# The closing pass of a four-layer graph network moved into the blocks of its last graph convolution

## What is computed

```python
def gcn_conv(x, src, dst, W, b):            # dinv = 1/sqrt(degree)
    h = x @ W
    msg = h[src] * (dinv[src] * dinv[dst])[:, None]
    return segment_sum(msg, dst) + b
# h3 is the layer's normalised input, x3 the residual stream
x_out = x3 + gcn_conv(relu(gcn_conv(h3, ..., W1, b1)), ..., W2, b2)   # 64 -> 32 -> 64 features
```

## Time and profile before

| | |
|---|---|
| median of 3 runs | 7401.49 us (7392.78 to 7404.23) |
| profiled execution, span from first to last instruction | 7386.2 us |
| DVE / PE / GpSimd / ACT busy over the span | 61 / 63 / 51 / 22 % |
| mean granted TensorE clock | 0.816 of full speed |
| second graph convolution, first sums to last addition | 6716.4 to 7214.6 us |
| closing pass | 7214.6 to 7386.2 us |

### The profile page before, as it was taken

One profiled execution on the slowest core, in us unless ns is written; L12 is line 12 of the kernel. 1 busy time (PEld: TensorE's weight loads), 2 busy tenths in 40 slices (PEclk: granted clock), 3 DMA queues, 4 the chain that ended last, 5 costly groups with the idle time before them and its releaser, 6 DMA issues. The chain is left out here.

```text
span 7386.2 us, 101314 instructions
## 1 busy us (share of the span) xinstructions
PE 4675.6 (63%) x31722; PEld 4192.0 (57%) x31722; DVE 4503.1 (61%) x5720; ACT 1623.3 (22%) x2242; POOL 3795.4 (51%) x3348
## 2 busy tenths in 40 slices
PE   4665335760188785555555866666668774784797
PEld 2354334650177785555555866666568774674675
DVE  6998443222577786666667842232398894683457
ACT  0143112330143343222222421111134340000001
POOL 0198565563277403777771047777600006766766
PEclk9866668995599998766767987777789996997899
DMA  2298666656722374332333753334357883122009
GB/s 75 48 276 259 140 147 140 138 108 201 252 73 73 101 245 154 83 79 79 81 78 101 249 164 109 109 109 112 100 186 250 304 307 112 49 59 91 14 12 278
DMA packets 837873, 1024.59 MB, mean 139 GB/s; under 512 B 589119, under 2 KB 601812, under 8 KB 836380
## 3 DMA queue, kind: packets, MB, share of 16 engines
q1 hardware_dynamic: 534716, 742.63, 31.5%
q0 software_dynamic: 144256, 90.12, 8.3%
q10 hardware_dynamic: 158560, 187.31, 7.6%
HBM read 608.19 MB, written 417.84 MB: 139 GB/s over the span
## 5 line engine op out<-in xcount | busy, mean ns | idle before, releaser
L839 POOL DMA_INDIRECT gc_msgs<-t,src_rows x784 | 754.4, 962 | 1098.1 <-POOLq L146 804.2
L893 POOL DMA_INDIRECT acc<-de_sums,de_put x392 | 608.5, 1552 | 410.9 <-DMA acc<-de_sums,de_put 263.5
L1913 PEld LDWEIGHTS gc_ring<-gc_msgs,gc_hot 128*128 128x128 f32 x4736 | 628.4, 210 | 305.9 <-issue 298.1
L1913 PE MATMUL gc_ring<-gc_msgs,gc_hot 128*128 x4736 | 654.9, 297 | 230.4 <-SPq L1872 229.3
L839 POOL DMA_INDIRECT at2s_ends<-h,src_rows x392 | 369.9, 944 | 533.6 <-POOLq L146 414.4
L839 POOL DMA_INDIRECT at1s_ends<-x,src_rows x392 | 389.2, 993 | 490.5 <-POOLq L146 371.3
L1027 PE MATMUL de_ring<-de_win,de_pick 128*128 x2368 | 343.2, 305 | 272.7 <-DMA de_win<-t 272.7
L1027 PEld LDWEIGHTS de_ring<-de_win,de_pick 128*128 128x128 f32 x2368 | 322.9, 217 | 295.0 <-issue 289.1
L839 POOL DMA_INDIRECT at1s_ends<-x,dst_rows x392 | 419.0, 1069 | 119.5 <-issue 119.5
L839 POOL DMA_INDIRECT re_rows<-x,src_rows x392 | 406.5, 1037 | 125.1 <-issue 124.8
L1393 PE MATMUL re_psR<-w_rel,re_own 128*128 128x128 f32 x3136 | 398.6, 293 | 73.6 <-DVE re_own L1330 73.3
(11 more groups left out here) (471 smaller groups left out, 11359.4 us busy)
## 6 DMA issues: line engine op xcount, KB each, us to landing
rew_win<-x SPq DMA_DIRECT2D x74, 544.0 KB, 4.0
at1w_win<-g SPq DMA_DIRECT2D x74, 544.0 KB, 4.0
at2w_win<-g SPq DMA_DIRECT2D x74, 544.0 KB, 4.0
de_near<-same SPq DMA_DIRECT2D x74, 512.0 KB, 5.1
de_win<-t SPq DMA_DIRECT2D x74, 512.0 KB, 4.6
x<-rew_win SPq DMA_DIRECT2D x74, 512.0 KB, 2.9
h<-at1w_win SPq DMA_DIRECT2D x74, 512.0 KB, 2.9
h<-at2w_win SPq DMA_DIRECT2D x74, 512.0 KB, 2.9
```

What stands on the lines that cost most here:

```text
L839: nc.gpsimd.indirect_dma_start(buf[:, t * width:(t + 1) * width], None, table, bass.IndirectOffsetOnAxis(ap=rows[:, t:t + 1], axis=0)).the ...
L893: nc.gpsimd.indirect_dma_start(g.acc0[j % 2], bass.IndirectOffsetOnAxis(ap=put[:, j:j + 1], axis=0), sums[:, j * D:(j + 1) * D], None, com ...
L1913: done = nc.tensor.matmul(ring[:, bass.ds(to[n], SLOT)], hot[k][:, n, :], each_group(msgs[:, bass.ds(of[n], MID)], SLOT // MID), start=Fal ...
```

## The change

- `skip_dense` adds the last bias `bg2` to `x` on GpSimd, after `centred`; ACT's store of `x3` waits for it (`biased`).
- `gcn_last` takes the place of `gcn_edges("gc2")` and of `gcn_close`. It does the same 74 blocks. The ring is now two halves of 8 slots (2 banks each), cleared by ACT instead of PE; PSUM also holds one transposed and one widened block. Per iteration m, PE does the sums of block m, transposes the 16 tiles that are finished after block m-1, and widens the ones transposed before; DVE does hot(m), two half additions of block m-1, the scaling by `dinv`, and `close(m-1)`; ACT clears two halves, evacuates the transposes, loads an `x` block and stores a closed one. A block of 16 tiles starts where the path stands, so tiles at the seam may be written twice, in order.
- The output is laid out by partition; the host puts it in node order.
- `setup` makes the slot addresses of the halves and two more columns of `g.blocks` (six small DVE operations).

```diff
+++ setup
+                link(v.tensor_scalar(half[:, 0:HALF], at[:, 0:HALF], float(SLOT), None, ALU.mult))
+                link(v.tensor_scalar(half[:, HALF:S], at[:, HALF:S], at[:, HALF:HALF + 1], None, ALU.subtract))
+                link(v.tensor_scalar(half[:, HALF:S], half[:, HALF:S], float(SLOT), float(HALF * SLOT), ALU.mult, ALU.add))
...
+++ skip_dense
+            @block.gpsimd
+            def _(pool):
+                def bias(b):
+                    s = b.slot
+                    held(pool, centred, b.number + 1, g.passed)
+                    nc.gpsimd.tensor_tensor(grouped(x[s][:, :], D), grouped(x[s][:, :], D), each_group(g.w["bg2"][:, :], J), ALU.add).then_inc(biased, 1)
+                pipeline(pool, bias, slots=DEEP)
...
-                    act.wait_ge(centred, b.number + 1)
+                    act.wait_ge(biased, b.number + 1)
...
+++ gcn_last, ACT
+                def clear(unit):
+                    if unit >= 2:
+                        act.wait_ge(added, unit - 1)
+                    nc.scalar.activation(ring[:, unit % 2 * BUF:(unit % 2 + 1) * BUF], blank[:, :], ACT.Copy).then_inc(zeroed, 1)
...
+                for m in range(BLOCKS + 1):
+                    if m < BLOCKS:
+                        clear(2 * m)
+                        clear(2 * m + 1)
+                    if m >= 1:
+                        turn(m)
+                    if m >= 2:
+                        if m + 1 <= BLOCKS:
+                            load(m + 1)
+                        store(m - 1)
+                store(BLOCKS)
...
+++ gcn_last, PE
+                def turn(m):
+                    pe.wait_ge(scaled, m)
+                    if m >= 2:
+                        pe.wait_ge(evac, m - 1)
+                    transpose_pairs(nc, psT, u[m % 2], g.ident, S // 4).then_inc(turned, 1)
+
+                def widen(m):
+                    pe.wait_ge(evac, m)
+                    if m >= 2:
+                        pe.wait_ge(ready, m - 1)
+                    times(nc, psH, uT[m % 2], g.w["gcn2"], S // 4).then_inc(product, 1)
+
+                for m in range(BLOCKS):
...
+                    pe.wait_ge(hot_made, m + 1)
+                    need = pe.value_load(g.blocks[m:m + 1, 1:2], min_val=1, max_val=STEPS)
+                    pe.wait_ge(arrived, need)
+                    for n in range(S):
+                        if n % HALF == 0:
+                            pe.wait_ge(zeroed, 2 * m + n // HALF + 1)
+                        done = nc.tensor.matmul(ring[:, bass.ds(to[n], SLOT)], hot[m % 2][:, n, :],
+                                                each_group(msgs[:, bass.ds(of[n], MID)], SLOT // MID),
+                                                start=False, stop=(n % HALF == HALF - 1), skip_group_check=True)
+                        if n % HALF == HALF - 1:
+                            done.then_inc(summed, 1)
+                    if m >= 1:
+                        turn(m)
+                    if m >= 2:
+                        widen(m - 1)
+                turn(BLOCKS)
+                widen(BLOCKS - 1)
+                widen(BLOCKS)
...
+++ gcn_last, DVE
+                def close(m):
+                    dve.wait_ge(x_in[m % 3], 16 * ((m - 1) // 3 + 1))
+                    dve.wait_ge(product, m)
+                    v.tensor_tensor(x[m % 3][:, :], x[m % 3][:, :], psH[:, :], ALU.add).then_inc(ready, 1)
+
+                for m in range(BLOCKS + 1):
+                    if m < BLOCKS:
+                        if m >= 2:
+                            dve.wait_ge(summed, 2 * (m - 1))
+                        v.tensor_tensor(hot[m % 2][:, :, :], each_group(fixed[:, 0:P], S), spread(g.steep[:, m * S:(m + 1) * S], P),
+                                        ALU.is_equal).then_inc(hot_made, 1)
...
+                    for h, col in enumerate((0, 6)):
+                        unit = 2 * (m - 1) + h
...
+                        dve.wait_ge(summed, unit + 1)
...
+                        v.tensor_tensor(grouped(window, MID), grouped(window, MID),
+                                        grouped(ring[:, h * BUF:(h + 1) * BUF], SLOT)[:, :, 0:MID], ALU.add).then_inc(added, 1)
...
+                    v.tensor_tensor(grouped(u[m % 2][:, :], MID), grouped(ended, MID), dinv, ALU.mult).then_inc(scaled, 1)
+                    if m >= 2:
+                        close(m - 1)
+                close(BLOCKS)
```

More of the change, by code:

```diff
@@ L1956, in _, with gcn_last @@
                         nc.vector.scalar_tensor_tensor(grouped(o[:, :], MID), grouped(o[:, :], MID), 0.0, dinv, ALU.max, ALU.mult).then_inc(done_made, 1)
[L1959 to L1971, removed]
-        with nc.Block() as block:
+def gcn_last(nc, g, nodes, acc, out):
+    W = B * MID
+    BUF = HALF * SLOT
+    with Room(nc, g, "gc2") as r:
+        msgs = r.sb("msgs", [P, T * MID])
+        hot = [r.sb(f"hot{k}", [P, S, P]) for k in range(2)]
+        blank = r.sb("blank", [P, BUF])
+        x = [r.sb(f"x{k}", [P, S * D]) for k in range(3)]
+        u, uT = ([r.sb(f"{n}{k}", [P, S * MID]) for k in range(2)] for n in ("u", "uT"))
+        ring, fixed = r.ps("ring", [P, 2 * BUF]), r.ps("fixed", [P, 512])
+        psT, psH = r.ps("psT", [P, S * MID]), r.ps("psH", [P, S * D])
+        got = [r.sem(f"got{k}") for k in range(4)]
+        x_in = [r.sem(f"x_in{k}") for k in range(3)]
+        acc_in, done_out = r.sem("acc_in"), r.sem("done_out")
+        arrived, blanked, hot_made, zeroed, summed, added, link_s, scaled, turned, evac, product, ready = (r.sem(n) for n in (
+            "arrived", "blanked", "hot_made", "cleared", "summed", "added", "link", "scaled", "turned", "evac", "product", "ready"))
+        with nc.Block() as block:
+            @block.gpsimd
+            def _(pool):
+                for b in range(STEPS):
+                    if b >= 4:
+                        held(pool, arrived, b - 3, g.passed)
+                    gather(nc, msgs[:, b * W:(b + 1) * W], nodes, g.src_rows[:, b * B:(b + 1) * B], got[b % 4])
@@ L1973, in _ @@
             @block.sync
             def _(sp):
[L1975 to L1980, removed]
+                for k in range(4):
+                    part = slice(k * (PITCH // 4) * MID, (k + 1) * (PITCH // 4) * MID)
+                    sp.dma_start(acc[:, part], nodes.rearrange("(p t) d -> p (t d)", t=PITCH)[:, part]).then_inc(acc_in, 16)
@@ L1982, in _ @@
             @block.vector
             def _(dve):
[L1984 to L2018, removed]
-                        act.dma_start(out[CHUNK * (STEPS - 1):N - LAST_REST, :].rearrange("(j p) d -> p j d", p=P),
-                                      grouped(x[b.slot][:, 0:LAST_FULL * D], D)).then_inc(last_out, 16)
-                        act.dma_start(out[N - LAST_REST:N, :], x[b.slot][0:LAST_REST, LAST_FULL * D:(LAST_FULL + 1) * D]).then_inc(stored[b.slot], 16)
-                        act.wait_ge(last_out, 16)
-                    else:
-                        act.dma_start(whole[b.number], grouped(x[b.slot][:, :], D)).then_inc(stored[b.slot], 16)
-                def landed(b):
-                    act.wait_ge(stored[b.slot], 16 * b.nth)
-                    act.sem_inc(free, 1)
-                pipeline(act, order=[(0, turn), (2, store), (4, landed)], slots=DEEP)
@@ L2031, in _ @@
-            @block.gpsimd
-            def _(pool):
-                def bias(b):
-                    s = b.slot
-                    held(pool, x_in[s], 16 * b.nth, g.passed)
-                    nc.gpsimd.tensor_tensor(grouped(x[s][:, :], D), grouped(x[s][:, :], D), each_group(g.w["bg2"][:, :], J), ALU.add).then_inc(biased, 1)
-                pipeline(pool, bias, slots=DEEP)
+                v = nc.vector
+                link = Link(dve, link_s)
+                v.memset(blank[:, :], 0.0).then_inc(blanked, 1)
```

82 lines of the change are left out of this document (74 added, 8 removed).

## The result

The changed kernel takes 7851.99 us (median of 4 runs, 7848.21 to 7854.65) against 7402.86 (7392.78 to 7418.66) before: a ratio of 1.0598, with an interval of 1.058 to 1.0616. It is slower by 449 us, and the forecast was 7853.

A forecast was written before the change was run, and what follows sets the result against it. PE, and early the gathers, bounded the convolution. In the changed kernel a ring through PE, DVE and ACT: 6743.0 + 965.6 + 23 + 1.7 + 105 = 7838, plus 15.3: 7853 us; range 7810 to 7896, for 8 in 10 7700 to 7905.

The forecast's parts named there:

- The ring: gcn_last: close, comparison, addition, clear, sums, transposes and product follow one another, 11.8 us, 13.6 with clock; 71 blocks 965.6 us.
- The clock: gcn_last: PE's idle of 5.2 us per block lowers its granted clock afterwards, costing 1.8 us a block.
- The exclusion: skip_dense: POOL's bias addition starts first and holds small multiplication L1830 for 2.2 us, 48 times: +105 us.
- the reading of L752: Dense stage: L752, said to have two SBUF operands, ran 1.22 us undisturbed inside a POOL addition; by it alone, 0 us.
- the ring without the exclusion: Rival: gcn_last's ring as forecast, but L1830 in skip_dense not held by POOL; 7753 us, chance 0.37.
- The tail: End of gcn_last: last sums, transposes, products, closes, additions, clock and final store take 23 us.
- The new operations of the setup: setup: six small DVE operations, each near 0.17 us plus a gap, +1.7 us (0 to 3).
- ACT's loads and stores: gcn_last: x loads and stores on ACT's queue, two issues of about 0.4 us per block, are hidden: 0.
- DVE has more than half of each block free: Second graph convolution before the change: only PE and, early, the gathers set the pace; ACT is wholly free.
- The offset of 15.3 us: Whole kernel: median of the runs lies 15.3 us above the profiled span, kept and added to 7838 for 7853.
- The low-clock rival: gcn_last: low clock for much of PE's work, 16 us a block, +170, about 8020 us; chance 0.06.
- The faster rival: gcn_last: comparison and close overlap PE's sums, so a block costs 7.5 us; 7313 us, chance 0.04.

The follow-up runs named there:

- PE kept busy: Changed kernel plus 20 products of zeros on PE at the start of each last-stage block, in its idle time: 7738.52 us.
- the comparison ahead: Changed kernel with DVE making the comparison for block m+1 before close(m-1) instead of after it: 7669.47 us.
- the run with one input: Changed kernel with skip_dense's 16-element multiplication by dinv replaced by a reciprocal with one SBUF operand: 7760.66 us.
- The kernel with the ring opened: Changed kernel with DVE doing close(m-2), then comparison m+1, and ACT loading x for m and storing m-2: 7445.06 us.
- the last one: The kernel with the ring opened, plus skip_dense's bias waiting for the previous chunk's result and ACT's x store one step deeper: 7352.54 us.

## Why the prediction was right, and which step of it was wrong

**The ring** was right in order and size: 13.6 us forecast, 13.67 in the block shown and 13.62 in the mean. From the close to the start of the sums it was taken as 5.15 us and took 5.09 (7406.98 to 7412.07). Two errors cancel in PE's part. At full clock it was taken as 6.6 us (4.0, 0.60, 1.99) and takes 6.11 from the sums to the next close (7305.66 to 7311.77, with PE kept busy). Some 0.2 of these 0.5 us lie in the 4.0 us of the sums, which the prediction says leave out the blanking of the ring: the one product at L1912 stands between the 24 and the 8 instructions of the earlier trace rows, and without it 32 take 3.83 us. The clock was taken as 1.8 us and cost 2.5 in the block shown (8.58 us from 7412.07 to 7420.65, less 6.11). That 13.6 was met so closely is in this part luck. The tests by order are the stronger evidence: with the comparison ahead 182 us go, with the close deeper too 407 go.

**The exclusion** was right in size: 105 forecast, 100.1 measured, because the wait is 2.06 us longer per chunk and not 2.2. In six chunks POOL led by 0.02 us and the multiplication took 2.37, as forecast; in the 42 others it started 0.18 us after DVE's end, not 0.29, and led by 0.13.

**The step that was wrong** is the reading of L752. The prediction says that it had "also two SBUF operands" and that it does not agree with the rule of the Trainium skill (SBUF — State Buffer, "SBUF: two separate sides"). It had one in SBUF and one in PSUM. By that rule a GpSimd operation that reads SBUF and a DVE operation with two SBUF inputs exclude each other, and the one that starts second waits; every row here agrees: L761, L1987 and L1844 held, L752 held in both runs that put its operand in SBUF, and free with it in PSUM. L1994 and L1848, with one operand in PSUM, are free too. The chance of 0.37 for the ring without the exclusion rested on that misreading and on the near tie of the starts; with the right one the case against 105 us would have been only the question who starts first. It did not spoil the forecast, because the value was taken from L761, the nearest row.

**The rest.** The tail took 24.8 us (23 forecast). The new operations of the setup cost about 1 us where they stand (1.7 forecast): from L482 to the first write of the first dense stage's `cen` it takes 223.2 to 223.8 us in the three traces without them and 223.9 to 225.0 in the seven with them. ACT's loads and stores and the longer output rows were taken as 0, and no wait of the stage names them; the output rows alone were shown to be worth nothing. The difference of the spans is 460.2 us (452 forecast), of which 10.6 belong to neither part and have no shown cause. The prediction's sentence that DVE has more than half of each block free holds for the mean of the stage (212 of 498 us busy) and not for the late block of the earlier trace rows, where it works 2.98 of 5.29 us; nothing in the sum hangs on it. The offset of 15.3 us was too large a correction: the span of the profiled execution after lies only 5.6 us under the median of its runs. The forecast of the span was 8 us too low and the offset 10 us too high, so that the errors cancel to 1 us in the median, which is luck.

**The rivals.** The ring without the exclusion is measured by the run with one input: 7760.66, against 7753 worked out. The low-clock rival fell (13.6 us a block and not 16, with a granted clock of 0.75 in the stage). The faster rival's condition, that neither comparison nor close holds PE, was not met by this order. The kernel with the ring opened and the last one meet it: the comparison lies under PE's sums and the close beside ACT's clear. Its 7313 us left out the 105 of the exclusion, although nothing in the rival removes it: with the term the same sum gives 7418, and the kernel with the ring opened, which has the exclusion, took 7445.

**What stays open.** Why every second block in the run with PE kept busy still has its sums at a lower clock; what the 10.6 us before skip_dense are; and what a version would give in which PE never idles. Putting the small multiplication's operand in PSUM, which would free it without any reordering, was not tried.

## What to carry to other kernels

Before a pass is folded into a pipelined loop, write down for each engine's queue what stands ahead of what, and follow one block around: if the walk passes through several engines and comes back to the first with nothing beside it, its lengths add up (here 13.6 us, though no engine has more than 6.6 us of work at full clock), and one more iteration of depth is the remedy. An operation moved to an idle engine can cost on the busy one: look which of its neighbours read two SBUF operands, and read in the allocation where each operand lies, since the profile's row does not tell. A lead of 0.02 to 0.15 us at the start decided such a case in 48 chunks of 49, so it should be set by a wait and not left to chance.

## What the runs showed of the hardware that was not expected

- A DVE operation of 16 elements a partition, 0.17 us long, took 2.27 us beside a GpSimd addition of 2.36. The loss is what is left of the other's addition (2.1 us here), whatever its own work; L752 with its operand in SBUF, which is longer and starts further into an addition, lost 1.4 us.
- The exclusion of L752 depends on where the second input lies, and neither on how it is repeated nor, for L1987, on the size of its tensor: 1.22 us with 16 columns in PSUM, 2.60 with 16 or with 32 columns in SBUF.
- Twenty products of zeros per block, 3.41 us of PE's time, made the kernel 113 us faster, by giving the sums after them more clock (3.83 us in every second block and 5.46 in the others, instead of 6.31).
